# The edge stage of a graph-network kernel: first weights split on VectorE, third-sweep sources copied, sums begun ahead of keys, words loaded inside root products, lower counts spread

## The reference, cut to what matters

```python
edge_index = jnp.stack([src, dst])
x = _layernorm(x + L0(x, edge_index, edge_type_4, ...))   # 3 relational layers, 4 relations and a root each
x = _layernorm(x + L1(x, ...))                            # 2 GCN layers
x = _layernorm(x + L2(x, edge_index, ...))                # 2 attention layers, 4 heads and 1
x = _layernorm(x + L3(x, edge_index, ...))                # 2 attention layers, 8 heads and 1

def rgcn_conv(x, weight, root, bias, src, dst, etype):
    out = x @ root + bias
    for r in range(4):
        sel = etype == r
        deg = zeros(n).at[dst].add(sel)
        norm = where(sel, 1 / maximum(deg[dst], 1), 0)
        out = out + segment_sum((x @ weight[r])[src] * norm[:, None], dst, n)
    return out
```

## Time and profile before

| | us |
|---|---|
| median of 3 runs | 1507.03 |
| lowest, highest | 1502.5, 1509.78 |
| the profiled execution, its own time | 1506.79 |
| its span, first to last instruction | 1505.1 |

### The profile page before, as it was taken

One profiled execution on the slowest core, in us unless ns is written; L12 is line 12 of the kernel. 1 busy time (PEld: TensorE's weight loads), 2 busy tenths in 40 slices (PEclk: granted clock), 3 DMA queues, 4 the chain that ended last, 5 costly groups with the idle time before them and its releaser, 6 DMA issues.

```text
span 1505.1 us, 22367 instructions
## 1 busy us (share of the span) xinstructions
PE 1394.8 (93%) x7674; PEld 1295.0 (86%) x7674; DVE 786.9 (52%) x1847; ACT 428.6 (28%) x928; POOL 556.2 (37%) x625
## 2 busy tenths in 40 slices
PE   5999799999999999999999899889998999788797
PEld 3676799999999999999999898879978987677784
DVE  7867655323544346564231534646374614599744
ACT  2543522101110010110100311245574334445432
POOL 8101322424242534425424242033434454345630
PEclk9989899999999999999999999999999999967799
DMA  3110111112335223342111211122102211200001
GB/s 112 53 32 24 36 37 32 58 37 74 90 95 148 64 85 110 90 126 71 55 43 51 65 48 39 47 70 63 53 22 60 87 42 37 74 1 1 1 11 52
DMA packets 57782, 86.47 MB, mean 57 GB/s; under 512 B 6447, under 2 KB 54438, under 8 KB 57563
## 3 DMA queue, kind: packets, MB, share of 16 engines
q1 hardware_dynamic: 45184, 65.82, 14.8%
q10 hardware_dynamic: 12504, 19.36, 4.2%
HBM read 83.24 MB, written 1.92 MB: 57 GB/s over the span
## 4 chain that ended last, share of the span: by engine, by line
PE 75%; DVE 14%; ACT 4%; POOL 3%; issue 3%; DMA 2%; DVEq 0%; ACTq 0%; SPq 0%; POOLq 0%
PE psum L2399 14%; PE psum L2402 13%; PE psum L2403 13%; PE psum L2416 8%; PE psum L2419 8%; PE psum L2859 5%; DVE max_scratch L2104 2%; PE psum L2517 2%; PE psum L2464 2%; POOL w_lo L908 2%; PE psum L2909 1%; PE psum L2760 1%; PE psum L2764 1%; PE psum L2765 1%; PE psum L2388 1%
## 5 line engine op out<-in xcount | busy, mean ns | idle before, releaser
L2399 PE MATMUL psum<-w_lo,xT_hi 128*125 128x384 f32 (+5 forms) x1200 | 414.3, 345 | 7.2 <-DVE x_nat L1830 2.2
L2402 PE MATMUL psum<-w_hi,xT_lo 128*125 128x384 f32 (+5 forms) x1200 | 408.5, 340 | 0.0
L2403 PE MATMUL psum<-w_hi,xT_hi 128*125 128x384 f32 (+5 forms) x1200 | 408.2, 340 | 0.0
L895 POOL CAST w_hi<-w_raw 128x384 fp32r<-128x384 f32 x190 | 105.1, 553 | 501.5 <-PE psum L2403 495.4
L2399 PEld LDWEIGHTS psum<-w_lo,xT_hi 128*125 128x125 f32 (+1 forms) x1200 | 227.2, 189 | 11.8 <-POOL w_lo L908 3.4
L2402 PEld LDWEIGHTS psum<-w_hi,xT_lo 128*125 128x125 f32 (+1 forms) x1200 | 227.1, 189 | 0.5
L2403 PEld LDWEIGHTS psum<-w_hi,xT_hi 128*125 128x125 f32 (+1 forms) x1200 | 226.5, 189 | 0.0
L1673 DVE TENSOR_TENSOR h_lo<-psum,h_hi 125x384 fp32r<-125x384 f32 (+1 forms) x120 | 66.9, 558 | 289.2 <-ACT h_hi L1068 288.2
L1068 ACT ACTIVATE h_hi<-psum 125x384 fp32r<-125x384 f32 (+1 forms) x120 | 58.9, 491 | 536.4 <-PE psum L2403 532.0
L2416 PE MATMUL psum<-h_lo,adjacency 125*125 125x384 f32 (+3 forms) x600 | 203.6, 339 | 4.1 <-DVE h_lo L1673 2.1
L897 POOL TENSOR_TENSOR w_lo<-w_raw,w_hi 128x384 fp32r<-128x384 f32 x190 | 201.5, 1061 | 15.2
(11 more groups left out here) (335 smaller groups left out, 2123.6 us busy)
## 6 DMA issues: line engine op xcount, KB each, us to landing
w_raw<-weights_dram SPq DMA_DIRECT2D x296, 192.0 KB, 2.4
score_w_raw<-weights_dram ACTq DMA_DIRECT2D x58, 192.0 KB, 2.7
x_nat<-x_dram SPq DMA_DIRECT2D x1, 1875.0 KB
x_residual<-x_dram SPq DMA_DIRECT2D x1, 1875.0 KB
score_a_rows<-L_gnn_a_src_dram ACTq DMA_DIRECT2D x8, 192.0 KB, 3.2
score_a_rows<-L_gnn_a_dst_dram ACTq DMA_DIRECT2D x8, 192.0 KB, 4.8
out_dram<-x_residual SPq DMA_DIRECT2D x4, 375.0 KB
rgcn_bias<-rgcn_bias_dram SPq DMA_DIRECT2D x1, 1125.0 KB
```

Of the source, the lines that this page charges most:

```text
L895: nc.gpsimd.tensor_copy(mem.wh[:, slot, :], mem.raw[:, raw_slot, :]).then_inc(w_hi_ready, 1)
L2399: ins = nc.tensor.matmul(o, h, wl, start=(j == 0), stop=False, skip_group_check=True)
L2402: nc.tensor.matmul(o, l, wh, start=False, stop=False, skip_group_check=True)
L2403: ins = nc.tensor.matmul(o, h, wh, start=False, stop=stop and j == k - 1, skip_group_check=True)
```

## The change: what it does

1. The lower parts of chunks 6 to 9 and 15 to 19 are made on VectorE at places in the plan: chunks 6 to 9 after tile (0, 27), 10 and 11 after (1, 10), 12 to 14 after (1, 25), 15 after (1, 40), 16 to 19 after (2, 27). `first_lower` on GpSimd is removed, and so is a wait of VectorE on it.
2. In the second sweep ScalarE copies the 44 source one-hots of the longer pair to the first 44 places, in four copies of 11 (`copy_sources`); the third sweep reads them at fixed addresses and waits for these copies. A padding column is set to zero at the start by GpSimd.
3. The start matmuls of the first sweep no longer wait for the first one-hot, except that of bank 0. Those of the later sweeps lose that wait too.
4. The words of the second and third sweep are loaded inside root products (0, 1) and (1, 1), one or two after the first matmul of each step; those of the first sweep at its start. `half` is no longer loaded on TensorE.
5. The last root product moves from after tile (2, 22) to after (2, 12). Between sweeps ScalarE rounds after the root's output and the first splits, not partly ahead of them. At the end it rounds block 1 ahead of the loop over blocks, and does `h_hi` ahead of `counts_cast`.
6. `broadcast_rows` and `rows_over` move ahead of the decoding of the third sweep; `counts_lo` of relation 0 is made block by block (block i at step i) and not for five blocks at step 3.

```diff
-        ROOTS_AFTER = ((8, 17, 26, 35), (14, 24, 34), (22,))
+        ROOTS_AFTER = ((8, 17, 26, 35), (14, 24, 34), (12,))
-        WEIGHTS_AFTER = {(0, 4): (RAW, RAW + 1), (1, 10): (WRING, 15)}
+        WEIGHTS_AFTER = {(0, 4): (RAW, RAW + 1), (0, 27): (RAW + 1, WRING), (1, 10): (WRING, 12), (1, 25): (12, 15),
+                         (1, 40): (15, 16), (2, 27): (16, 2 * WRING)}
+        COPY_AFTER = {(1, 15): (0, 11), (1, 25): (11, 22), (1, 36): (22, 33), (1, GROUP - 1): (33, GROUP)}
...
+            nc.gpsimd.memset(mem.oh_src[:, :, BP:BP + 1], 0.0)
...
-            first_lower(RAW + 1, WRING)
-            first_lower(15, 2 * WRING)
...
+            def copy_sources(a, e):
+                act.wait_ge(onehot_ready, GROUP + e)
+                act.wait_ge(source_ready, len(MADE_BY_ACT))
+                flat = mem.oh_src[:, :, :].rearrange("p t n -> p (t n)")
+                if not copied:
+                    act.wait_ge(consts_ready, 6)
+                    act.wait_ge(sweep_done, 1)
+                    act.wait_ge(place_ready, 1)
+                    copied.append(act.value_load(mem.word_i[0:1, 3 * GROUP_WORDS:], min_val=0, max_val=GROUP * (BP + 1)))
+                nc.scalar.activation(flat[:, a * (BP + 1):e * (BP + 1)],
+                                     flat[:, bass.ds(copied[0] + a * (BP + 1), (e - a) * (BP + 1))], ACT.Copy
+                                     ).then_inc(sources_copied, 1)
...
                     if last_sweep is not None:
-                        for m in range(2, NB):
+                        for m in range(NB):
                             read_odd(last_sweep, m)
...
                     if step[1] < SWEEPS - 1:
-                        read_odd(step[1], 0)
-                        read_odd(step[1], 1)
                         last_sweep = step[1]
...
-            counts_cast(0, 0)
+            read_odd(SWEEPS - 1, 1)
             for i in range(H_LAYER):
                 h_hi(i, i % NB, i)
                 if i < 4:
-                    for m in ((1,), (2, 3), (4,), ())[i]:
+                    counts_cast(0, i)
+                    for m in ((2,), (3, 4), (), ())[i]:
                         read_odd(SWEEPS - 1, m)
-                    counts_cast(0, i + 1)
+                    if i == 3:
+                        counts_cast(0, NB - 1)
...
+            added.append(dve.value_load(mem.added_i[0:1, 0:1], min_val=0, max_val=2))
+            rows_over()
+            dve.wait_ge(sweep_done, SWEEPS)
...
+            decode(SWEEPS - 1, 0)
...
                     if i < 4:
                         decode(SWEEPS - 1, i + 1)
-                    if i == 1:
-                        rows_over()
+                        counts_lo(0, i)
                     if i == 3:
-                        for m in range(NB):
-                            counts_lo(0, m)
+                        counts_lo(0, NB - 1)
...
+            def early(f, m, load):
+                pe.wait_ge(early_read, f * NB + m)
+                o = bank(7, 0, HW)
+                for j in range(KC):
...
+                    ins = nc.tensor.matmul(o, h, wl, start=(j == 0), stop=False, skip_group_check=True)
...
+                    if load:
+                        load_words(2 if j == 0 else 1)
+                    nc.tensor.matmul(o, l, wh, start=False, stop=False, skip_group_check=True)
+                    ins = nc.tensor.matmul(o, h, wh, start=False, stop=(j == KC - 1), skip_group_check=True)
...
+            def begin_first():
+                pe.wait_ge(place_ready, 1)
+                load_words(GROUP_WORDS)
+                pe.wait_ge(consts_ready, 6)
+                pe.wait_ge(xT_lo_ready, UNITS)
+                for b in (5, 6, 1, 2, 3, 4):
+                    begin_bank(b)
+                pe.wait_ge(onehot_ready, 1)
+                begin_bank(0)
...
-                if s < PAIRS:
-                    sources = mem.oh_src[:, n, 0:BP]
-                else:
-                    sources = mem.oh_src[:, :, :].rearrange("p t n -> p (t n)")[:, bass.ds(half[0] + t * (BP + 1), BP)]
+                if s == PAIRS and t in COPIES:
+                    pe.wait_ge(sources_copied, COPIES.index(t) + 1)
+                sources = mem.oh_src[:, n if s < PAIRS else t, 0:BP]
...
-                    if step[1] == BATCHES - 2:
-                        load_words()
...
-                    if step[1] < SWEEPS - 1 and step[2] == 20:
-                        load_words()
...
+            broadcast_rows()
+            pe.wait_ge(sweep_read, (SWEEPS - 1) * READS + 2)
...
-                    if l == 0 and f == 0 and i == 0:
-                        broadcast_rows()
```

More of the change, by code:

```diff
@@ L406, in program @@
         apart_ready = sem("apart_ready")
+        sources_copied = sem("sources_copied")
         source_ready = sem("source_ready")
@@ L540, in adjacency_plan @@
                         out.append(("weights",) + WEIGHTS_AFTER[s, t])
+                    if (s, t) in COPY_AFTER:
+                        out.append(("copy",) + COPY_AFTER[s, t])
                     if t in ROOTS_AFTER[s]:
@@ L878, in _ @@
             place_tiles()
-            def first_lower(a, e):
-                for c in range(a, e):
-                    pool.wait_ge(w_hi_ready, c + 1)
-                    pool.wait_ge(w_lo_ready, c)
-                    nc.gpsimd.tensor_tensor(mem.wl[:, c % WRING, :], mem.raw[:, c % RAW, :],
-                                            mem.wh[:, c % WRING, :].bitcast(F32), ALU.subtract).then_inc(w_lo_ready, 1)
-            first_lower(RAW + 1, WRING)
-            first_lower(15, 2 * WRING)
             def split(c, slot, raw_slot, turn):
@@ L1107, in _ @@
                     sources(ACT_SOURCES[step[2]])
+                elif step[0] == "copy":
+                    copy_sources(*step[1:])
                 elif step[0] == "root":
@@ L1685, in _ @@
             nc.vector.tensor_reduce(mem.cand[0:BP, :], mem.flag[0:BP, :, :], AX.X, ALU.max).then_inc(cand_ready, 1)
-            dve.wait_ge(sweep_done, SWEEPS)
-            for t, v in ((mem.hh, 1.0), (mem.hl, 0.0)):
-                ins = nc.vector.memset(t[:, :, HW:HX].bitcast(F32), v)
-            link(ins)
-            added.append(dve.value_load(mem.added_i[0:1, 0:1], min_val=0, max_val=2))
-            decode(SWEEPS - 1, 0)
             chosen = []
@@ L1723, in rows_over @@
                 extra_columns()
+            added.append(dve.value_load(mem.added_i[0:1, 0:1], min_val=0, max_val=2))
+            rows_over()
+            dve.wait_ge(sweep_done, SWEEPS)
+            for t, v in ((mem.hh, 1.0), (mem.hl, 0.0)):
+                ins = nc.vector.memset(t[:, :, HW:HX].bitcast(F32), v)
+            link(ins)
+            decode(SWEEPS - 1, 0)
             def inverse_degrees(r):
@@ L2489, in _, with load_words @@
-            words, half = [], []
-            def load_words():
-                pe.wait_ge(place_ready, 1)
+            words = []
+            def load_words(n):
                 a = len(words)
                 words.extend(nc.values_load_multi_w_load_instructions(
-                    mem.word_i[0:1, a:a + GROUP_WORDS], engines=[mybir.EngineType.PE], min_val=0,
+                    mem.word_i[0:1, a:a + n], engines=[mybir.EngineType.PE], min_val=0,
                     max_val=512 * (8 ** DIGITS - 1) // 7)[1])
-                if len(words) == 3 * GROUP_WORDS:
-                    half.append(pe.value_load(mem.word_i[0:1, 3 * GROUP_WORDS:], min_val=0, max_val=GROUP * (BP + 1)))
+            def early(f, m, load):
+                pe.wait_ge(early_read, f * NB + m)
+                o = bank(7, 0, HW)
+                for j in range(KC):
+                    c = f * KC + j
+                    if m == 0:
+                        pe.wait_ge(w_lo_ready, c + 1)
+                    h, l, wh, wl = mem.xh[:, j, nodes(m)], mem.xl[:, j, nodes(m)], mem.wh[:, c % WRING, :], mem.wl[:, c % WRING, :]
+                    ins = nc.tensor.matmul(o, h, wl, start=(j == 0), stop=False, skip_group_check=True)
+                    if f == 1 and m == 0 and j == 0:
+                        ins.then_inc(w_used, 1)
+                    if load:
+                        load_words(2 if j == 0 else 1)
+                    nc.tensor.matmul(o, l, wh, start=False, stop=False, skip_group_check=True)
+                    ins = nc.tensor.matmul(o, h, wh, start=False, stop=(j == KC - 1), skip_group_check=True)
+                    if m == NB - 1 and j < KC - 1:
+                        ins.then_inc(w_used, 1)
+                ins.then_inc(early_root, 1)
@@ new lines, in begin_bank @@
+            def begin_bank(b):
+                w = TAIL if b == 6 else 512
+                nc.tensor.matmul(bank(b, 0, w), mem.init_rows[0:2, :], mem.init_cols[0:2, 0:w], start=True, stop=False,
+                                 skip_group_check=True)
+            def begin_first():
[7 more added lines that the diff above has]
+                begin_bank(0)
@@ L2501, in tile_sums, with begin_sweep @@
+            def begin_sweep(s):
```

(7 more changed lines are left out.)

22 lines of the change are left out of this document (3 added, 19 removed).

## The result

The changed kernel's median is 1485.81 us (4 runs, 1481.86 to 1487.21) beside 1504.76 us for the kernel before (4 runs). The ratio is 0.9876, with a 95% interval of 0.9852 to 0.9900: 19 us less, where the prediction had 25. Run again beside one of the experiments, it had a median of 1485.67 over 5 runs and a ratio of 0.9868 (0.9844 to 0.9893). The profiled execution, at 1481.86 with a span of 1480.0, is the fastest of its runs; its closeness to the predicted 1481.7 is chance, as the stage shows.

A forecast was written before the change was run, and what follows sets the result against it. TensorE, busy for 93% of the span, was taken as the bound. Gains of 5.5, 2.3, 4.0, 2.3, 8.1 and 2.9 summed to 25.1, taking 1506.79 to 1481.7, predicted as 1482; range 1473 to 1494.

The forecast's parts named there:

- C: Second sweep to the end of its first root product: 11.49 becomes 9.2, gain 2.3.
- H: Clock at the row picking and the product behind it: stays up with shorter idle time, gain 2.9, bounds 0 and 4.5.
- G: After the sweeps, last tile to row picking: 33.8 becomes 25.7, VectorE setting the pace; gain 8.1, bounds 5 and 9.0.
- A: First lower parts off GpSimd: VectorE's source one-hots speed up, first root product starts 2.0 earlier; bounds 0 and 2.7.
- the loads: Seven words loaded inside a root product: cost taken as 0.3, bounds 0 and 1.27.
- F: Third sweep: 23.2 becomes 20.9, with VectorE at 18.7 below TensorE; gain 2.3, bounds 0 and 4.5.
- B: Second sweep's words moved into a root product: nine tiles and a root took 9.55 against 5.74 undisturbed; gain 3.5.
- D: Second sweep's next ten tiles and root product: 10.37 becomes 6.4, gain 4.0, of which the standstill is 2.41.
- VectorE becomes the bound: Rival: TensorE still waits twice for VectorE in the second sweep and the clock falls; gain 17.5, 1489; chance 0.19.
- The copies: ScalarE's four source copies for the third sweep: about 1.4 each, 5.6 in all, while ScalarE is nearly idle.
- The slower rival: Rival: register-addressed copies on ScalarE make the kernel slower than before, needing 12 for each copy; chance 0.02.
- issue is no bound: Rival: tiles go at VectorE's pace, not held by TensorE's issue; gain 29.6, 1477; chance 0.12.

The follow-up runs named there:

- Late chunks: Changed kernel with the lower parts of chunks 16 to 19 made after the third sweep: that sweep takes 19.9 in place of 22.8, picking starts at 164.47.
- The fixed place: Changed kernel with all words loaded in the sort and each tile's PSUM bank fixed in the program (counts not those of the edges): third sweep 19.7.
- the words at the old place: Changed kernel with words of the second and third sweep loaded after tile 20 of the first two sweeps, as before: 1485.87 in one execution.

## Why the prediction came out as it did

The total lay in the range, but not because the parts did. The sum for the stage was 25.1 and the stage gave 20.0. C and H came as put and G by its upper bound; A, the loads and F had their mechanism wrong. Two things hid part of these misses in the total, and that is luck: G gave 1.5 more than put, and the kernel before came out 2.3 lower in the result than in the three runs that the forecast started from.

- **Loads inside the roots (in B and D).** The step that failed is "I take 0.3, since the loads that stood between sort products ... left no gap of their own". Seven words a root were taken at 0.3 and cost 1.91 and 2.64, 4.0 too little in the sum. The upper bound of 1.27 was the old standstill, which is not the price of the loads but, by my reading, what was left of 2.9 us of sequencer after the tiles that were prepared ahead. That price stood in the trace of before, in the rows of the sequencer shown above, and I did not read them. During the sort the same loads cost nothing: with all words there the start matmuls begin at 51.31, and at 51.37 after. B without A came to 1.96 of 3.5, and D to 1.53 of 4.0.
- **A.** 1.46 of 2.0, but not by the mechanism put. "VectorE is the later engine there" was a misreading. In the kernel before the first eight tiles start 0.48 to 0.53 apart with TensorE never idle, at half clock, and the ninth destination one-hot is ready at 59.94, just in time. Source one-hots fell to 0.31 as put and the ninth destination one-hot is ready at 57.5, but the tiles still go at 0.53 until the clock rises. What moved is the start, which was put at "Nothing". Before:

```profile
53.12 2.92 PE L2486 MATMUL psum<-init_columns,init_rows 2*125 2x512 bf16 x7 [1.88 <-DVE onehot_dst L1618]
55.97 4.62 PE L2517 MATMUL psum<-onehot_dst,onehot_src 128*125 128x512 bf16 x18
```

  and after:

```profile
51.37 2.89 PE L2513 MATMUL psum<-init_columns,init_rows 2*125 2x512 bf16 x7 [0.52 <-issue]
```

  The start matmuls begin 1.75 earlier and the tiles 1.77. The early start needs the lower parts off GpSimd: with them back the nine tiles end at 60.51, and before at 60.59. The lower parts off GpSimd without the early start were not run; by the spacing of the tiles they would have given next to nothing. The lower bound named for this term, TensorE's issue, is not what held it: the half clock is.
- **C.** 2.28 of 2.3; the working held step by step.
- **F.** 0.44 of 2.3. What failed is "I put it at 18.7, below TensorE": VectorE's 20.2 less ten one-hots made ahead is 17.2, so the sum held some 1.5 for waits at a full ring and took the rest as work that can be done at any time. It idled for 2.60 while the ring was full and was late behind tile (2, 27), by the four lower parts and by GpSimd's split. Late chunks show TensorE's own sweep at 19.9, a us below the 20.9 that I worked out. So the rival "VectorE becomes the bound" was right for the third sweep alone. The pace of 0.48 was right for tiles that are not prepared.
- **The copies.** 1.36 for eleven sources, as worked out (1.4), nowhere on the path. The slower rival never came near its point of 12.
- **G.** 9.63 of 8.1. The picking started 24.21 behind the last tile, with no idle time ahead of it and 0.5 in all from the last tile on, where the working had 25.7 by VectorE and 24.8 by TensorE. TensorE's sum was the bound. VectorE was faster than put because a lower count alone takes 0.87 where the five of the earlier trace rows took 1.24:

```profile
151.80 0.87 DVE L1766 SCALAR_TENSOR_TENSOR edge_counts_lo<-edge_counts,count_offset,adjacency 125x626 fp32r<-125x626 int16 x1
...
163.76 2.65 DVE L1766 SCALAR_TENSOR_TENSOR edge_counts_lo<-edge_counts,count_offset,adjacency 125x626 fp32r<-125x626 int16 x2
```

  The two at 163.76 take 1.3 each and lie beside GpSimd's splits of later weights.
- **H.** 2.69 of 2.9. The window of the picking, against the earlier trace rows:

```profile
166.40:168.00 1.60, 1.60 (x9) 1.31 (x8) 1.57 (x4) 1.60 (x1) 1.60 (x2) 1.00 0.20 73
```

The misses add up: 4.0 for the loads, 0.5 for A and 1.9 for F, less 1.5 for G, and 0.2 for H: 25.1 - 5.1 = 20.0. Of what would show it right, the idle times (1.31 in the third sweep), the last tile (142.26, not 134 to 138) and the clock throughout failed; a "third sweep of 23" and "tiles of 0.5 right after the two roots with loads" were named as signs that it was wrong, and both came (22.8; 0.46 and 0.50).

The rival "issue is no bound" falls: only with the place fixed do tiles go at 0.30. The Trainium skill (TensorE: Matmul & The Clock Gate, section "Wait — 56ns, not 53.3ns?") gives about 62 ns of sequencer time for a matmul where it is not decoded in hardware, so by it two matmuls alone would not be held up by their issue. The fixed place agrees (0.30 a tile); the 0.16 of register work for each tile is not in that figure.

## What to carry to other kernels

A load into a register costs the sequencer of its engine, and that price stands in the trace by line even where the engine shows no gap; moving it inside a stretch where the array is busy hides it only in part (0.2 to 1.3 us in a root product here), so put it where no prepared work depends on the sequencer, as in the sort. A sum of an engine's work against another's is a bound only if the work can be done when there is time for it: a full ring makes an engine idle first and late afterwards. And compare stages by a place in the trace right behind them, since here the unchanged rest of the kernel moved by 6 us from one execution to the next. Before a stretch is put down to a late engine, hold the spacing of its tiles against that of the same work at the other clock.

## What the runs showed of the hardware that was not expected

The length of a wait alone did not tell whether the clock falls. After an idle time of 1.27 the kernel before ran at 0.50, from 73.65 on, while with the words at the old place TensorE stood for 1.28 at the same tile and kept 1.00:

```profile
72.00:75.00 3.00, 3.00 (x18) 2.61 (x17) 1.77 (x7) 0.73 (x2) 0.00 (x0) 1.00 0.01 3
75.00:77.00 2.00, 2.00 (x15) 1.72 (x14) 0.37 (x2) 0.64 (x2) 0.00 (x0) 1.00 0.00 0
```

It also stayed at 1.00 after the 2.53 of `rows_over` back at step 1, and fell within the 3.95 of the lower counts in one piece. In the changed kernel's third sweep, after waits of 1.31, 0.64 and 0.61, it was 0.50 for some 3 us:

```profile
138.00:139.00 1.00, 1.00 (x5) 0.72 (x4) 1.00 (x4) 0.00 (x0) 0.00 (x0) 0.50 0.01 2
139.00:140.00 1.00, 1.00 (x5) 0.64 (x4) 1.00 (x5) 0.00 (x0) 0.00 (x0) 0.50 0.05 16
```

Some six tiles that were paced by their registers at 0.45 went at 0.53 there, so that fall cost about 0.5. In the run with the fixed place, with waits of 1.27, 0.78, 0.60 and 0.53 at these tiles, it stayed at 1.00.
